# Two banks by turns for the weighted values, six for every other tile, statistics ahead of the constants and more filler matmuls in a two-layer transformer

## Chip, cores and metric

One NeuronCore of one Trainium2 chip (trn2). The metric is the device time of one execution, in microseconds (us), and the median over runs is what counts. The chip's engines are TensorE (PE), VectorE (DVE), ScalarE (ACT), GpSimd (POOL) and SyncE (SP, which here only issues DMAs).

## What is computed

Eight sequences of 1024 tokens, 256 wide, go through two layers, each with 16-head causal attention (heads of 16) and a feed-forward part, all with a residual and a layer norm ahead. Cut to its bones:

```
for layer in (0, 1):
    x = x + softmax(causal(q k^T / 4)) v @ w_out      # q, k, v from layernorm(x); layer 1 also turns q, k (rope)
    x = x + ffn(layernorm(x))
# ffn of layer 0: gates from entmax of 16 logits, z = (x W) * gate, gelu between two such products
# ffn of layer 1: shared squared-relu expert of 128; routed experts only where a gate reaches 1
```

## The kernel before, in words

**Tiles and units.** Tokens are worked in blocks of 512 (c = 0 or 1 of each sequence b), keys in tiles of 128. Attention is cut into 128 units u = (b, layer, group of 4 heads, c), four units to a pass (b, layer, c). For a unit PE first makes scores "s" by query rows (line 1116, with the mask added by a matmul at line 1121 where tiles are packed), DVE takes their maxima (lines 1723 and 1726), POOL splits the maxima into three bf16 parts (line 1651 on), PE turns these ("mt", line 1129), ACT copies them (line 1462) and SP writes them by DMA into the stack of operands. Then PE makes the scores again by key rows, with the maximum subtracted ("st", line 1141), ACT takes the exponential into `probs` (line 1455), POOL cuts the diagonal (line 1630), and PE weighs the values ("pv", line 1159) into one accumulator, `o_bank`. ACT copies this out (line 1468), PE turns it ("nm", line 1167), DVE divides by the sum (line 1745).

**Banks.** PSUM has eight banks of 512 columns. Bank 5 is the accumulator; the other seven (`BANKS`) are a pool, handed to every other tile by turns. `claim` in PE's program waits until the tile that had the bank before is read out (semaphores `drained`). `weigh_values` waits at j = 0 until the copy of the unit before has left the accumulator (`o_drained`). A set-up stage on banks 0 to 4 folds weights (lines 1280 to 1302, with DVE's copies at line 1884) before the attention starts.

**Order.** `program_order` is a planner: it runs over a model of the engines, with a time for each step (`TIMES`), a list of when each bank comes free, at most four "s" tiles and three "st" tiles open, and chooses PE's next step by rank. `LEAD`, `DENSE` and `SPREAD` say when the scores of a coming unit count as late. Steps of the feed-forward chains, of projections (line 1088 and 1096) and of loads go between attention steps. All engines run this one order, each its own part of it.

**Fillers.** Where the model has PE idle (`gap`) before some tiles, the table `FILL` gives the number of dummy matmuls, gap / 0.25, that PE issues into the claimed bank before it waits for the tile's data (`keep_going`, line 1058). Before, this is done for the first tile kinds "xt", "yt", "at" (transposes of x, y and the gates' weights) and for the first "st" of a unit. The profile has 178 fillers.

**The start.** SP issues the first two blocks of x (line 927), with the weights of layer 0 between them, then 3 MB and more of weights that are folded. DVE clears small tiles, fills `vaug` with ones (line 1899), three stacks `stk_k` with -1 (line 1901) and the accumulator with 0 (line 1902), raises `ready0`, and then takes the statistics of both blocks of x ("stat", lines 1692 to 1701). POOL makes the inverse root (line 1593), ACT the normalised x (line 1404), PE its transposes (line 1076), then projections and values, which ACT copies into `vaug` (line 1444), and SP stores and loads the stacks (line 954 on). PE waits for `ready0` at 2 at the end of the set-up stage, ACT at its first copy of values of (0, 0, 0).

Of the kernel before, what the change touches and what calls it, by code (L numbers as in the profile page):

```python
# [10 lines left out]
P = 128  # L11
# [7 lines left out]
DH = D // H  # L19
# [23 lines left out]
PBUF = 4  # L43
PRING = 4
QRING, SRING = 4, 2
O_BANK = 5
LEAD = 9.0
PACE = 0.9
DENSE = 2.0
SPREAD = 1.0  # L50
# [1 line left out]
FOLD_LOADS = 3 + 2 + 10  # L52
SETUP_COPIES = (11, 10)
PACK_S, PACK_T = True, True
BANKS = (0, 1, 2, 3, 4, 6, 7)
SETUP_BANKS = 5
S_MOST, ST_MOST = 4, 3
MARGIN = 2.0
# [174 lines left out]
class Plan:  # L233
# [203 lines left out]
    def weighing_time(self, u, j):  # L437
        b, l, g, c = UNITS[u]
        values = [("v", b, l, j // TPC, tp) for tp in range(TPC // 2)] if g == 0 else []
        if j == key_tiles(c)[-1] and u > 1:  # L440
            values.append(("nm", u - 2))
        if any(item not in self.at for item in values):
            return None
        return max([self.steps[u, j], self.out.get(u - 1, 0.0) if j == 0 else 0.0] + [self.at[item] for item in values])

    def pair_time(self):

# [55 lines left out]
def program_order():  # L503
# [21 lines left out]
    while main or todo or any(plan.chains) or plan.held or plan.outputs:  # L525
# [65 lines left out]
        if can:  # L591
            time, rank, what, args = min(can, key=lambda choice: choice[1])
        else:
            time, rank, what, args = min(choices, key=lambda choice: choice[0])
            plan.pe = max(plan.pe, time) + (0.001 if what == "wait" else 0.0)
            gap += plan.pe - now
        if what == "wait":
            pass
        elif what == "chain":
            item = plan.chains[args[0]][0][0][0]  # L600
            if item[0] in ("xt", "yt", "at") and gap > FILL_TIME:
                FILL[item] = int(gap / FILL_TIME)
            given[args[0]] += plan.give(args[0])
        elif what == "st":
            u, j, h = main.pop(0)
            if j == 0 and h == 0:
                begins[u] = plan.pe
            if j == 0 and h == 0 and gap > FILL_TIME:
                FILL["st", u, j, h] = int(gap / FILL_TIME)
            plan.scores_t(u, j, h)  # L610
            position += 1
            c = UNITS[u][3]
            line = starts[u] + DENSE * unit_work(u) * (j * HG + h + packed_t(j, c)) / (HG * len(key_tiles(c)))
            a, z = query_range(j, c)
            passed += packed_t(j, c) * (2 * (z - a) / 2400 + 0.05)
        else:
            what()
        if what != "wait":
            gap = 0.0

    order = plan.order
# [7 lines left out]
RANK = dict(mt=1, nm=2, burst=3, late=4, st=5, pair=5.5, due=6, s=7, chain=8, single=10)  # L629
EARLY = True  # L630

FILL_TIME = 0.25
FILL = {}

PLACE = {}
# [82 lines left out]
def x_slot(b, c):  # L718
    return (NC * b + c) % X_SLOTS
# [8 lines left out]
def transformer_kernel(nc, x_d, w_qkv_d, w_out_d, proj_d, c1_d, win1_d, wout1_d, c2_d, win2_d, wout2_d,  # L728
# [3 lines left out]
    with ctx:  # L732
# [89 lines left out]

        ps = ctx.enter_context(nc.psum_tensor("ps", [P, 8 * BANK], F32))
        bank = [ps[:, BANK * b:BANK * (b + 1)] for b in range(8)]
        o_bank = bank[O_BANK]
        t_bank = [bank[b] for b in BANKS]

        def sem(name):
# [90 lines left out]
        def _(sp):  # L919
# [20 lines left out]
                sp.dma_start(k2_d[b][l][heads, :, cols].rearrange("h d t -> (h d) t"), src[:, 2]).then_inc(stored, 16)  # L940

            def load_stack(u):
                b, l, g, c = UNITS[u]
                for k in range(c + 1):
                    for w in range(2):
                        parts_in_dram(sp, PROJ["qk", b, l, k, g // 2, w])
                if u >= NBUF:
                    written(sp, last_transposed(u - NBUF, key_tiles(UNITS[u - NBUF][3])[-1]))
                loaded, i, n = stk_loaded[u % NBUF], u % NBUF, BANK * (c + 1)
                heads = slice(HG * g, HG * (g + 1))  # L950
                q = q_d[b][l][heads, :, :, BANK * c:BANK * (c + 1)]
                for r in range(2):
                    rows = slice(ROWS_T * r, ROWS_T * (r + 1))
                    sp.dma_start(stk_q[rows, i], q.rearrange("h d p t -> (d p) h t")).then_inc(loaded, 16)
                    k = k_d[b][l][r, heads, :, :, 0:n].rearrange("h d p t -> (d p) h t")
                    sp.dma_start(stk_k[rows, i, :, 0:n], k).then_inc(loaded, 16)
                sp.dma_start(stk_q[ROWS_A:ROWS_S, i], q[:, :, 0, :].rearrange("h d t -> d h t")).then_inc(loaded, 16)
                k = k2_d[b][l][heads, :, 0:n].rearrange("h d t -> d h t")
                sp.dma_start(stk_k[ROWS_A:ROWS_S, i, :, 0:n], k).then_inc(loaded, 16)
# [86 lines left out]
        def _(pe):  # L1046
# [62 lines left out]
            def score(u, i, h, p):  # L1109
                c, slot = UNITS[u][3], u % NBUF  # L1110
                width = dict(score_parts(i))[p]
                pe.wait_ge(stk_loaded[slot], 16 * STACK_DMAS * (u // NBUF + 1))
                n, (out, done) = packed(width), claim(("s", u, i, h, p))
                for a in range(n):
                    q = stk_q[0:ROWS_S, slot, h + a, P * i - BANK * c:P * (i + 1) - BANK * c]
                    ins = pe.matmul(out[:, width * a:width * (a + 1)], q, stk_k[0:ROWS_S, slot, h + a, BANK * p:BANK * p + width],  # L1116
                                    start=a == 0, stop=a == n - 1 and n == 1)
                if n > 1:
                    last = out[:, 0:n * width].rearrange("q (a w) -> q a w", a=n)[:, :, width - P:width]
                    mask = mask_b[:, BANK - P:BANK].rearrange("q (a w) -> q a w", a=1).broadcast_to([P, n, P])  # L1120
                    ins = pe.matmul(last, ident_b[:], mask, start=False, stop=True)  # L1121
                ins.then_inc(done, 1)

            def max_rows(u):
                pt, done = claim(("mt", u))
                rows = pt[0:NP * HG, 0:BANK // 2].bitcast(BF16)
                pe.wait_ge(mx_ready, u + 1)
                for i in range(TPC):
                    ins = pe.transpose(rows[:, P * i:P * (i + 1)], mparts[:, i].rearrange("q p h -> q (p h)"), ident_b[:])  # L1129
                ins.then_inc(done, 1)  # L1130

            def scores_t(u, j, h):
                c, slot = UNITS[u][3], u % NBUF
                out, done = claim(("st", u, j, h))
                if j == 0 and h == 0:
                    keep_going(("st", u, j, h), out)
                    pe.wait_ge(m_loaded, 16 * (MT["mt", u] + 1))
                a, z = query_range(j, c)
                cols, width = slice(a - BANK * c, z - BANK * c), z - a
                for k in range(packed_t(j, c)):  # L1140
                    ins = pe.matmul(out[:, width * k:width * (k + 1)], stk_k[0:ROWS, slot, h + k, P * j:P * (j + 1)],  # L1141
                                    stk_q[0:ROWS, slot, h + k, cols], start=True, stop=True)
                ins.then_inc(done, 1)

            def weigh_values(u, j):
# [2 lines left out]
                    pe.wait_ge(p_ready, DIAGONAL[u, j])  # L1148
                else:
                    in_sbuf(pe, last_transposed(u, j))  # L1150
                if j == 0 and u:
                    pe.wait_ge(o_drained, u)
                if g == 0 and j % TPC == 0:
                    for tp in range(TPC // 2):
                        in_sbuf(pe, ("v", b, l, j // TPC, tp))
                a, z = query_range(j, c)
                cols, v = slice(a - BANK * c, z - BANK * c), v_slot(b, l, j // TPC)
                for h in range(HG):
                    ins = pe.matmul(o_bank[32 * h:32 * h + DH + 1, cols], vaug[:, v, j % TPC, HG * g + h, :],  # L1159
                                    probs[:, STEP[u, j] % PBUF, h, cols], start=j == 0, stop=j == key_tiles(c)[-1])  # L1160
                ins.then_inc(pv_done, 1)

# [26 lines left out]

            def narrow_product(key, n, b, c, w):
                need_xT(n, b, c)
                pt, done = claim(key)
                for kd in range(KD):
                    for t in range(TPC):
                        ins = pe.matmul(pt[STRIP * t:STRIP * (t + 1), 0:P], w[:, kd, :], xT(n, b, c, kd)[:, P * t:P * (t + 1)],
                                        start=kd == 0, stop=kd == KD - 1)
                ins.then_inc(done, 1)
# [183 lines left out]
        def _(act):  # L1382
# [53 lines left out]
            def copy_v(item):  # L1436
                b, l, c, tp = item[1:]
                old = values_before(b, l, c)
                if old and tp == 0:
                    act.wait_ge(pv_done, PV["pv", LAST_UNIT[old], TT - 1] + 1)  # L1440
                if (b, l, c, tp) == (0, 0, 0, 0):
                    act.wait_ge(ready0, 2)
                pt = arrived(act, item)
                act.activation(vaug[:, v_slot(b, l, c), 2 * tp:2 * tp + 2, :, 0:DH],
# [19 lines left out]
            def copy_o(u):  # L1464
                act.wait_ge(pv_done, PV["pv", u, key_tiles(UNITS[u][3])[-1]] + 1)
                if u >= 2:
                    written(act, ("nm", u - 2))
                act.activation(oT[:, u % 2], o_bank, ACT.Copy).then_inc(o_drained, 1)  # L1468

            last_narrow = []  # L1470

# [207 lines left out]
        def _(dve):  # L1679
# [216 lines left out]
            dve.memset(up, 0.0).then_inc(up_zeroed, 1)  # L1896
            dve.memset(going[:, :, 1:E0], 1.0)
            dve.memset(going[:, :, 0:1], 0.0)
            dve.memset(vaug[:], 1.0)
            for i in range(NBUF):  # L1900
                dve.memset(stk_k[ROWS_A:P, i, :, :], -1.0)
            dve.memset(o_bank, 0.0)
            dve.wait_ge(pool_chain, 8)
            dve.drain().then_inc(ready0, 1)

            for item in ORDER:
                kind, *key = item
                if kind == "stat":
                    b, c = key
                    dve.wait_ge(x_loaded[x_slot(b, c)], 16 * ((NC * b + c) // X_SLOTS + 1))  # L1910
                    statistics(0, c, x[:, x_slot(b, c)], range(TPC))
                elif kind == "rot":
                    swap_pairs(*key)
                elif kind == "setup":
# [86 lines left out]
```

## Time and profile before

| | us |
|---|---|
| median of 3 runs | 3037.79 (3033.26 to 3039.56) |
| the profiled execution | 3033.58, of which the span is 3031.9 |
| PE busy | 2849.9 (94%), 17865 matmuls |
| DVE, ACT, POOL busy | 2074.2 (68%), 1957.8 (65%), 1213.8 (40%) |
| mean granted clock of TensorE | 0.978 |

### The profile page before, as it was taken

The numbers are of one execution on the slowest core, as the hardware profiler recorded it, in microseconds if no ns is written. First come the engines' busy times: TensorE is split into PE (matmuls) and PEld (weight loads), VectorE is DVE, ScalarE is ACT, GpSimd is POOL, SyncE is SP. The second block draws the span as 40 slices with busy tenths as digits, with TensorE's granted clock in tenths as the row PEclk, the third lists the DMA queues.
The fourth block names the chain that finished last, engine by engine and source line by source line (L and its number), as shares of the span: only waits on it lengthen the run. The fifth ranks groups of instructions, "written<-read, shape, count | busy, mean of one in ns | idle before, by whom it ended". The sixth has DMA issues, their size and how long they took to land.

```text
span 3031.9 us, 55430 instructions
## 1 busy us (share of the span) xinstructions
PE 2849.9 (94%) x17865; PEld 1365.7 (45%) x17865; DVE 2074.2 (68%) x5654; ACT 1957.8 (65%) x3868; POOL 1213.8 (40%) x2540
## 2 busy tenths in 40 slices
PE   5898999999999999999999999999999999999987
PEld 3334443445434454445534454344543445444533
DVE  3683677666877678685786758776687767867473
ACT  3465666776657766676667766577666776667544
POOL 2324461445415362263623545143531537225411
PEclk8899999999999999999999999999999999999989
DMA  5612452334423353234522435133442335333140
GB/s 170 147 27 67 97 112 48 86 99 110 98 56 87 93 125 88 55 104 90 143 56 56 128 86 123 38 88 96 114 108 42 96 96 131 71 63 80 45 105 16
DMA packets 241197, 268.27 MB, mean 88 GB/s; under 512 B 19568, under 2 KB 208912, under 8 KB 240912
## 3 DMA queue, kind: packets, MB, share of 16 engines
q1 hardware_dynamic: 240912, 264.66, 36.8%
q8 instruction: 156, 2.56, 0.4%
q14 instruction: 129, 1.06, 0.1%
HBM read 162.35 MB, written 100.66 MB: 87 GB/s over the span
## 4 chain that ended last, share of the span: by engine, by line
PE 70%; DVE 13%; ACT 8%; issue 3%; DMA 3%; SPq 2%; POOL 1%; DVEq 0%; ACTq 0%; POOLq 0%
PE ps L1159 16%; PE ps L1141 13%; PE ps L1116 12%; PE ps L1096 6%; PE ps L1088 6%; DVE mx L1726 5%; ACT probs L1455 4%; PE ps L1237 4%; PE ps L1232 3%; DMA stk_k<-k 3%; DVE ps L1723 2%; PE ps L1224 2%; PE ps L1076 2%; ACT xn L1404 1%; PE ps L1121 1%
## 5 line engine op out<-in xcount | busy, mean ns | idle before, releaser
L1455 ACT ACTIVATE probs<-ps 128x512 f32<-128x512 f32 (+1 forms) x2432 | 1229.4, 587 | 355.7 <-PE ps L1141 349.2
L1726 DVE TENSOR_REDUCE mx<-ps 128x1 f32<-128x512 f32 (+2 forms) x1408 | 886.9, 682 | 240.5 <-PE ps L1116 177.7
L1630 POOL TENSOR_SCALAR_AFFINE_SELECT probs<-probs 128x128 f32<-128x128 f32 (+2 forms) x1408 | 476.1, 345 | 1277.0 <-ACT probs L1455 1247.7
L1723 DVE CUSTOM_DVE_ANT_0 ps<-ps,mask_b 128x512 f32<-128x512 f32 (+1 forms) x1024 | 614.1, 649 | 316.0 <-PE ps L1116 313.5
L1116 PE MATMUL ps<-stk_k,stk_q 112*128 112x512 bf16 (+3 forms) x3072 | 771.5, 333 | 34.5 <-DVE mx L1726 11.7
L1141 PE MATMUL ps<-stk_q,stk_k 115*128 115x512 bf16 (+3 forms) x3072 | 751.4, 328 | 16.7 <-ACT probs L1455 9.2
L1159 PE MATMUL ps<-probs,vaug 128*17 128x512 f32 (+3 forms) x6144 | 580.6, 490 | 15.4 <-POOL probs L1630 10.2
L1141 PEld LDWEIGHTS ps<-stk_q,stk_k 115*128 115x128 bf16 x3072 | 270.6, 97 | 436.4 <-issue 220.1
L1116 PEld LDWEIGHTS ps<-stk_k,stk_q 112*128 112x128 bf16 x3072 | 276.2, 98 | 399.3 <-issue 251.3
L1159 PEld LDWEIGHTS ps<-probs,vaug 128*17 128x17 f32 x6144 | 137.0, 96 | 324.6 <-issue 203.5
L1088 PE MATMUL ps<-turned,wqkv 128*128 128x512 f32 x512 | 263.7, 610 | 6.8 <-ACT turned L1391 3.7
L1404 ACT ACTIVATE xn<-x,shift,rstd 128x256 f32<-128x256 f32 x256 | 138.4, 608 | 56.0 <-POOL shift L1595 56.0
L1615 POOL TENSOR_TENSOR scratch<-scratch,parts 128x512 f32<-128x512 f32 x128 | 148.2, 1158 | 57.2 <-ACT scratch L1422 29.0
L1620 POOL TENSOR_TENSOR parts<-scratch,parts 128x512 bf16<-128x512 f32 x128 | 147.9, 1158 | 47.0 <-ACT parts L1434 47.0
L1750 DVE TENSOR_TENSOR x<-ps,x 128x512 f32<-128x512 f32 x128 | 87.7, 686 | 112.4 <-PE ps L1096 112.3
L1468 ACT ACTIVATE oT<-ps 128x512 f32<-128x512 f32 x128 | 76.8, 600 | 135.2 <-PE ps L1159 135.2
L1391 ACT ACTIVATE turned<-ps 128x512 f32<-128x512 f32 x192 | 115.1, 614 | 60.6 <-PE ps L1175 42.4
L1462 ACT ACTIVATE mT<-ps 12x512 bf16<-12x512 bf16 x128 | 74.1, 579 | 122.2 <-PE ps L1129 122.1
L1482 ACT ACTIVATE scratch<-ps 128x512 f32<-128x512 f32 x128 | 75.3, 596 | 115.5 <-PE ps L1232 115.4
L1237 PE MATMUL ps<-scratch,win 128*128 128x512 f32 x256 | 132.6, 600 | 11.5 <-ACT scratch L1482 11.5
L1723 DVE DVE_READ_ACCUMULATOR2_ANT mx<- 128x1 f32 x1024 | 143.2, 140 | 0.0
L1096 PE MATMUL ps<-wo,turned 128*128 128x256 f32 x512 | 132.0, 386 | 6.6 <-ACT turned L1391 6.6
(153 smaller groups left out, 3005.4 us busy)
## 6 DMA issues: line engine op xcount, KB each, us to landing
k<-parts SPq DMA_DIRECT2D x128, 384.0 KB, 3.4
stk_q<-q SPq DMA_DIRECT2D x256, 192.0 KB, 4.1
stk_k<-k SPq DMA_DIRECT2D x128, 384.0 KB, 6.3
q<-parts SPq DMA_DIRECT2D x64, 384.0 KB, 3.0
stk_k<-k SPq DMA_DIRECT2D x128, 192.0 KB, 4.2
x<-in_L_attn_x SPq DMA_DIRECT2D x16, 512.0 KB, 5.0
k<-parts SPq DMA_DIRECT2D x64, 128.0 KB, 3.4
stk_q<-q SPq DMA_DIRECT2D x128, 64.0 KB, 6.4
```

The source lines that it names most:

```text
L1088: ins = pe.matmul(pt, wqkv[l][:, kd, D * w + P * m:D * w + P * (m + 1)], xT(2 * l, b, c, kd), start=kd == 0, stop=kd == KD - 1)
L1096: ins = pe.matmul(pt[:, D * i:D * (i + 1)], left(kd)[:, cols], right(kd), start=kd == 0, stop=kd == n_k - 1)
L1116: ins = pe.matmul(out[:, width * a:width * (a + 1)], q, stk_k[0:ROWS_S, slot, h + a, BANK * p:BANK * p + width], start=a == 0, stop=a == n ...
L1141: ins = pe.matmul(out[:, width * k:width * (k + 1)], stk_k[0:ROWS, slot, h + k, P * j:P * (j + 1)], stk_q[0:ROWS, slot, h + k, cols], star ...
L1159: ins = pe.matmul(o_bank[32 * h:32 * h + DH + 1, cols], vaug[:, v, j % TPC, HG * g + h, :], probs[:, STEP[u, j] % PBUF, h, cols], start=j ...
L1237: pe.matmul(acc, win2[:, k, :], hsb[k % 3], start=k == 0, stop=k == OC - 1)\
L1404: ins = act.activation(xn[:, t, :], src[:, t, :], ACT.Identity, bias=shift[:, i, t:t + 1], scale=rstd[:, i, t:t + 1])
L1455: act.activation(probs[:, step % PBUF, h:h + k, cols], src, ACT.Exp, scale=SCALE)\
L1615: pool.tensor_tensor(q, q, parts[:, o % PRING, 0], ALU.subtract).then_inc(rest_ready, 1)
L1630: pool.affine_select(out=diag, in_=diag, compare_op=ALU.is_ge, fill=0.0, base=0, pattern=[[0, k]] * (k > 1) + [[1, P]], channel_multiplier ...
L1723: dve.tensor_tensor_reduce(tile, tile, mask_b[:, BANK - width:BANK], 1.0, LOWEST, ALU.add, ALU.max, most)\
L1726: dve.tensor_reduce(most, tile.rearrange("q (k w) -> q k w", k=k), AX.X, ALU.max)\
```

## The change

The accumulator becomes two banks, 5 and 0, by the parity of the unit, and the wait at j = 0 is for the copy of the unit before the last. Bank 0 leaves the pool, which has six. The planner's rule for "pv" follows, and `LEAD` goes from 9 to 10. The constants that DVE writes move into a function that is called behind the statistics of block (0, 1); SP then waits for `ready0` at 2 ahead of the first stack, and ACT at the first values of both blocks. Fillers are planned before nine kinds of tile where the modelled gap is over 0.7 (before: four kinds, over 0.25), with the same division by 0.25; of the nine, "nm" has no `keep_going` in PE's program. In `score` and `narrow_product` the bank is now claimed before the wait for the operands.

```diff
-O_BANK = 5
-LEAD = 9.0
+O_BANKS = (5, 0)
+LEAD = 10.0
-BANKS = (0, 1, 2, 3, 4, 6, 7)
+BANKS = (1, 2, 3, 4, 6, 7)
...
-        return max([self.steps[u, j], self.out.get(u - 1, 0.0) if j == 0 else 0.0] + ...)
+        return max([self.steps[u, j], self.out.get(u - 2, 0.0) if j == 0 else 0.0] + ...)
...
-            item = plan.chains[args[0]][0][0][0]
-            if item[0] in ("xt", "yt", "at") and gap > FILL_TIME:
-                FILL[item] = int(gap / FILL_TIME)
...
-            if j == 0 and h == 0 and gap > FILL_TIME:
-                FILL["st", u, j, h] = int(gap / FILL_TIME)
...
         if what != "wait":
+            item = plan.order[made]
+            if gap > FILL_FROM and item[0] in ("xt", "yt", "at", "st", "mt", "s", "nm", "lg", "rt"):
+                FILL[item] = int(gap / FILL_TIME)
...
-FILL_TIME = 0.25
+FILL_TIME, FILL_FROM = 0.25, 0.7
...
             def load_stack(u):
+                if u == 0:
+                    sp.wait_ge(ready0, 2)
...
             def score(u, i, h, p):
+                n, (out, done) = packed(width), claim(("s", u, i, h, p))
+                keep_going(("s", u, i, h, p), out)
                 pe.wait_ge(stk_loaded[slot], 16 * STACK_DMAS * (u // NBUF + 1))
-                n, (out, done) = packed(width), claim(("s", u, i, h, p))
...
             def max_rows(u):
                 pt, done = claim(("mt", u))
+                keep_going(("mt", u), pt)
...
-                if j == 0 and u:
-                    pe.wait_ge(o_drained, u)
+                if j == 0 and u > 1:
+                    pe.wait_ge(o_drained, u - 1)
...
             def narrow_product(key, n, b, c, w):
+                pt, done = claim(key)
+                keep_going(key, pt)
                 need_xT(n, b, c)
-                pt, done = claim(key)
...
-                if (b, l, c, tp) == (0, 0, 0, 0):
+                if (b, l, tp) == (0, 0, 0):
                     act.wait_ge(ready0, 2)
...
-            dve.memset(vaug[:], 1.0)
-            for i in range(NBUF):
-                dve.memset(stk_k[ROWS_A:P, i, :, :], -1.0)
-            dve.memset(o_bank, 0.0)
-            dve.wait_ge(pool_chain, 8)
-            dve.drain().then_inc(ready0, 1)
+            def fill_constants():
+                dve.memset(vaug[:], 1.0)
+                for i in range(NBUF):
+                    dve.memset(stk_k[ROWS_A:P, i, :, :], -1.0)
+                for pt in o_bank:
+                    dve.memset(pt, 0.0)
+                dve.wait_ge(pool_chain, 8)
+                dve.drain().then_inc(ready0, 1)
...
                     statistics(0, c, x[:, x_slot(b, c)], range(TPC))
+                    if (b, c) == (0, 1):
+                        fill_constants()
```

## Rows read from the trace of the kernel before

**Rows 1.** Mean granted clock, then stretches: PE, PEld, DVE, ACT, POOL busy, PEclk, DMA.
```profile
...
core 0: 3031.9 us, clock 0.978
...
0.00:160.00 160.00, 116.19 (x633) 59.88 (x633) 82.53 (x191) 66.96 (x129) 51.60 (x106) 0.86 0.59 154
160.00:2880.00 2720.00, 2611.28 (x16514) 1255.08 (x16515) 1911.44 (x5265) 1822.28 (x3603) 1137.50 (x2367) 0.99 0.37 86
2880.00:3032.00 152.00, 122.48 (x720) 50.75 (x718) 80.18 (x201) 68.58 (x138) 24.71 (x68) 0.91 0.27 60
...
```

**Rows 2.** Timeline of DVE, start: start, length, engine, line, operation.
```profile
...
2.11 3.69 DVE L1899 MEMSET vaug<- 128x4352 f32 x1 [0.85 <-issue]
...
19.42 1.41 DVE L1692 BATCH_NORM_STATS2 st<-x 128x6 f32<-128x256 f32 x4
...
23.34 0.16 DVE L1701 TENSOR_SCALAR veps<-mv 128x4 f32<-128x4 f32 x1
...
61.11 0.69 DVE L1884 COPY probs<-ps 128x512 f32<-128x512 f32 x1 [37.61 <-PE ps L1280]
...
```

**Rows 3.** Timeline of all engines, start.
```profile
...
0.80 0.46 SPq L927 DMA_DIRECT2D x<-in_L_attn_x  x1
...
1.85 0.47 SPq L927 DMA_DIRECT2D x<-in_L_attn_x  x1
...
17.64 0.60 SPq L990 DMA_DIRECT2D scratch<-in_L_attn_Wv_up  x1
...
27.11 1.97 PE L1076 MATMUL ps<-ident,xn 128*128 128x128 f32 x8 [17.62 <-ACT xn L1404]
...
43.78 0.57 ACT L1444 ACTIVATE vaug<-ps 128x512 f32<-128x512 f32 x1
...
64.88 0.94 SPq L954 DMA_DIRECT2D stk_q<-q  x1
...
```

**Rows 4.** DMA issues of the first 60 us: count, KB each, time to landing.
```profile
...
x<-in_L_attn_x SPq DMA_DIRECT2D x2, 512.0 KB, 5.2
...
```

**Rows 5.** Stretches about the clock's changes, columns as in rows 1.
```profile
...
9.50:27.10 17.60, 0.00 (x0) 0.00 (x0) 12.04 (x24) 2.07 (x4) 1.22 (x2) 0.63 0.51 173
27.10:34.40 7.30, 6.55 (x14) 3.60 (x15) 0.00 (x0) 1.99 (x4) 0.00 (x0) 0.50 0.00 0
82.20:95.90 13.70, 8.71 (x28) 4.49 (x29) 9.28 (x32) 3.85 (x7) 2.05 (x6) 0.50 0.73 171
293.90:307.60 13.70, 8.23 (x26) 2.80 (x27) 13.22 (x59) 2.55 (x5) 2.06 (x6) 0.50 0.31 106
...
860.50:867.30 6.80, 6.80 (x16) 2.50 (x17) 5.80 (x16) 1.68 (x3) 0.00 (x0) 0.50 0.79 152
1222.30:1225.70 3.40, 3.40 (x8) 1.15 (x7) 3.06 (x9) 0.93 (x2) 0.00 (x0) 0.50 1.06 162
...
```

**Rows 6.** Timeline of PE at the seam of units 35 and 36.
```profile
...
855.22 0.41 PE L1159 MATMUL ps<-probs,vaug 128*17 128x128 f32 x8
856.44 0.63 PE L1167 MATMUL ps<-ident,oT 128*128 128x128 f32 x4 [0.81 <-ACT oT L1468]
...
859.27 0.38 PE L1129 MATMUL ps<-ident_b,mparts 128*12 128x128 bf16 x4 [0.84 <-POOL mparts L1654]
860.49 1.02 PE L1210 MATMUL ps<-ident,cum 128*48 128x128 f32 x4 [0.84 <-DVE cum L1822]
...
```

**Rows 7.** PE's waits, 160 to 2880 us: total, times, longest.
```profile
...
PE ps L1141 <- ACT probs L1455: 9.2, 28, 0.9
...
PE ps L1116 <- DVE mx L1726: 7.2, 27, 1.5
...
PE ps L1159 <- POOL probs L1630: 6.5, 8, 1.0
...
PE ps L1116 <- DVE mx L1723: 4.6, 12, 1.5
...
```

**Rows 8.** Timeline of PE near the end: fillers in one place.
```profile
...
3008.44 5.99 PE L1058 MATMUL ps<-mask_b,ident_b 128*128 128x512 bf16 x27
...
```

More of the change, by code:

```diff
@@ L443, in weighing_time @@
             return None
-        return max([self.steps[u, j], self.out.get(u - 1, 0.0) if j == 0 else 0.0] + [self.at[item] for item in values])
+        return max([self.steps[u, j], self.out.get(u - 2, 0.0) if j == 0 else 0.0] + [self.at[item] for item in values])
     def pair_time(self):
@@ L596, in program_order @@
             gap += plan.pe - now
+        made = len(plan.order)
         if what == "wait":
@@ L824, in transformer_kernel @@
         bank = [ps[:, BANK * b:BANK * (b + 1)] for b in range(8)]
-        o_bank = bank[O_BANK]
+        o_bank = [bank[k] for k in O_BANKS]
         t_bank = [bank[b] for b in BANKS]
@@ L1134, in scores_t @@
                 out, done = claim(("st", u, j, h))
+                keep_going(("st", u, j, h), out)
                 if j == 0 and h == 0:
-                    keep_going(("st", u, j, h), out)
                     pe.wait_ge(m_loaded, 16 * (MT["mt", u] + 1))
@@ L1158, in weigh_values @@
                 for h in range(HG):
-                    ins = pe.matmul(o_bank[32 * h:32 * h + DH + 1, cols], vaug[:, v, j % TPC, HG * g + h, :],
+                    ins = pe.matmul(o_bank[u % 2][32 * h:32 * h + DH + 1, cols], vaug[:, v, j % TPC, HG * g + h, :],
                                     probs[:, STEP[u, j] % PBUF, h, cols], start=j == 0, stop=j == key_tiles(c)[-1])
@@ L1467, in copy_o @@
                     written(act, ("nm", u - 2))
-                act.activation(oT[:, u % 2], o_bank, ACT.Copy).then_inc(o_drained, 1)
+                act.activation(oT[:, u % 2], o_bank[u % 2], ACT.Copy).then_inc(o_drained, 1)
             last_narrow = []
```

## The prediction

> **What bounds the kernel now.** I read first the mean granted clock and the span in three stretches [rows 1]: from 160 to 2880 us PE is busy 2611.3 of 2720.0 us, DVE 1911.4, ACT 1822.3. So PE is the bound, and in the long middle only 108.7 us of PE's idle time can be had. The two ends are worse: 43.8 us idle of the first 160, and 29.5 of the last 152. The same rows show the second reserve, the clock: 0.978 over all, 0.86 and 0.91 at the ends and 0.99 between. A share of 0.022 of 3031.9 us is 67 us, and that is what full clock would give back if PE had been busy all through the slow stretches.
>
> Then the timelines of the start. PE's first transpose of x is at 27.11 us, after 17.62 us of idle time that ended with the normalised x [rows 3]. DVE fills constants from 2.11 us and takes its first statistics at 19.42 us [rows 2], though both blocks of x were issued at 0.80 and 1.85 us and take 5.2 us to land [rows 3, 4]. So the statistics wait for DVE's queue, not for data.
>
> Then the clock by stretches [rows 5]. TensorE is at 0.50, which is 1.2 GHz, from 27.10 to 34.40 us, after 17.6 us without a matmul; for 13.7 us from 82.20 and again from 293.90; and once in each sequence's period of about 358 us for 6.8 us, as from 860.50 (3.4 us at 1222.30). There are seven of these dips; the five not shown, from 502.1, 1577.3, 1935.7, 2294.1 and 2652.5 us, are like the one at 860.50. Ahead of that one PE has idle pieces of 0.81, 0.84 and 0.84 us in 6 us, before "nm", before "mt" and before the transposes of the gates [rows 6].
>
> Last, PE's waits in the middle [rows 7]. This is where banks show. PE waits for a bank of the pool to be read out for 9.2 us in 28 waits before "st", and for 7.2 in 27 and 4.6 in 12 before scores: 21.0 us, 67 times, 0.31 us each. The list has 26 kinds of wait, and none is of the value matmuls (line 1159) for the copy of the accumulator (line 1468).
>
> **The change, part by part.** The sum goes by the profiled execution, 3033.6 us.
>
> *Statistics ahead of the constants.* Removed from the path to the first transpose: DVE's stretch from 2.11 to 19.42 us. The new limit is the landing of x: block (0, 0) at 0.80 + 5.2 = 6.0 us, block (0, 1) at 7.05. Both statistics take 19.42 to 23.50 us, 4.1 us [rows 2], so they end at 10.1 instead of 23.5: -13.4 us. What follows (inverse root, normalised x, transposes, projections, set-up) is one chain with no fixed time in it, and the last weights that set-up needs were issued at 17.64 us [rows 3], so I keep all of it. The constants themselves cost 17.3 us from 2.11 to 19.42 and one more bank of about 0.5 us, and end near 10.1 + 17.8 = 28 us. They are costed at nothing. Three covers hide them: DVE's next work is at 61.11 us after 37.61 us of idle time [rows 2]; ACT's first copy of values, behind the new wait, is at 43.78, now 30.4 us; and SP's first load of a stack, also behind the new wait, is at 64.88, now 51 [rows 3]. The nearest cover is ACT's, with 2.4 us to spare; if it is gone, the projections' copies queue behind it, and the cost is 1 to 3 us. Behind SP's wait stand only loads that come later anyway. PE issues the same first fillers, then is idle until about 13.7 us instead of 27.1. Whether the clock still falls is open: at worst the 7.3 us at 1.2 GHz stay, at best 6.55 / 2 = 3.3 us come back [rows 5]. I take 0. **-13.4.**
>
> *Fillers and the clock.* The new kinds are those at which PE idles ahead of the dips, "mt" above all [rows 6]. The idle 0.84 us before "mt" would be filled, the ones before "nm" (which has no filler in PE's program) and before the gates' transposes (where the model may see no gap) would not. The dips cost 6 x 6.8 + 3.4 = 44.2 us at half speed, 22.1 us [rows 5]. Between 0 and -22.1 I take half, -11, since one of three idle pieces goes. The two long stretches at 82 and 294 us have PE busy for 8.7 and 8.2 us at half clock, so at most 8.5 us come back; the 4 to 5 us of idle time at their heads are of kinds that get fillers, and I take -4. At the end, 0.09 of 152 us is 13.7 us of clock, half of it return; many fillers are there already, and the waits are for chains: -2. **-17.**
>
> Against it stand fillers that are too many. One costs 5.99 / 27 = 0.22 us [rows 8]. Where the trace has 0.84 us of idle time and the model should plan 2 us, seven fillers (at 0.25 us planned for each) take 1.55 us and make "mt" 0.7 us late, and behind "mt" on PE stand the gates' transposes, on ACT its copy, on SP the load of the maxima. One such place for each of 7 periods is 5 us; nothing at the least; three such places, 15 us. The old fillers of one or two before a unit's first "st" go, as their gaps are under 0.7. **+5.**
>
> *Two accumulators.* The wait that they loosen does not show in PE's list [rows 7], since the planner already puts other work there: at the seam of units 35 and 36 it makes "nm", scores, "mt" and transposes before any new value [rows 6]. An indirect gain cannot be more than the 6.5 us for which value matmuls wait for POOL. **0**, between -6.5 and 0.
>
> *Six banks in the pool.* The trace has no pool of six. From below: nothing or a small gain, if the new order places the tiles better. From above: the 21.0 us of waits for banks double. The steady need is less than seven: DVE reads a tile in 0.7 us and ACT in 0.6, PE makes one in 0.2 to 0.6, so two or three tiles in flight keep each busy; only bursts want the seventh. I take somewhat less than half of the 21.0. **+9.**
>
> *LEAD* 10 for 9 moves scores a little earlier and is costed at nothing, ±5 us; the bound is the 108.7 us of idle time in the middle, of which it can shift only the part at seams.
>
> Sum: 3033.6 - 13.4 - 17 + 5 + 9 = **3017 us** for a profiled execution. The median of before is 4.2 us above its own profiled execution, with runs on both sides; for a median I put 3018.
>
> **The rivals.**
> *1. Fillers bring nothing.* The pieces before "nm" and the gates' transposes are enough for the clock to fall, or the new order makes its gaps elsewhere. Then 3033.6 - 13.4 + 5 + 9 = 3034. For it: only one of three pieces is filled. Against: with it gone, PE's idle share of these 6 us is down by a third. Chance 0.18.
>
> *2. The pool of six bites; slower.* The place is where a chain holds a bank for long (the sum of eight gelu products, line 1237) while scores and "st" both want three or four. If waits for banks come to four times their number, that is 63 us more instead of 9: 3017 + 54 = 3071. It decides from 32 us on, since 3017 - 9 + 32 is past 3039.7. For it: the planner allows four scores and three "st" open, seven in all, against six. Against: now only 21 us in 2720 are spent so. Chance 0.08.
>
> *3. Turning through fewer banks costs clock.* Each short wait for a bank is an idle piece; if four more places of each period fall to 1.2 GHz for 6.8 us, that is 28 x 3.4 = 95 us, less for stretches where PE idles, say 3017 + 50 to 95 = 3067 to 3112. The trace speaks against it: the 67 waits for banks of the middle stand beside a clock of 0.99 [rows 1, 7]. Chance 0.03. The Trainium skill describes this in "TensorE: Matmul & The Clock Gate", section "A second HAM failure mode: psum-queue depth-cycling": a kernel that cycles through PSUM banks lets PE idle briefly so often that the clock goes up and down. By that rule the change would be slower; by the row it isn't.
>
> *4. All dips go and the accumulators help.* 3033.6 - 13.4 - 3.3 - 22 - 8 - 6 - 6.5 + 3 = 2977; with half of these, 2995. Chance 0.16.
>
> **How the numbers follow.** The forecast has 0.55. Its own range, by the bounds of fillers (0 to 15), banks (0 to 21) and dips (0 to -22), is 3000 to 3032. The range given adds rival 1 and the near half of rival 4, and the first part of rival 2: 2988 to 3040, which leaves out about 2 in 10. A difference of 0.2%, 6 us, is about what a measurement of this kernel can tell from none. Faster by more: the forecast, rival 4 and a third of rival 1: 0.77. Within: the rest of rival 1, 0.12. Slower: rivals 2 and 3: 0.11.
>
> **What would show it.** In the timeline of the start: statistics at 6 to 7 us, the first transpose at 13 to 14, the first copy of values near 30, set-up near 46. If the first transpose has moved by 13 and the middle hasn't gained, rival 1 is right. In the stretches: the seven dips, counted. In PE's waits: the waits of lines 1116 and 1141 for DVE and ACT, 30 us instead of 21; over 50 is rival 2. In the groups: fillers over 178, and what PE's busy time grows by. The forecast is wrong if the first transpose comes later than 16 us, or if the middle, from 160 us on, is longer than before.

## The result

The changed kernel takes 3055.79 us (median of 4 runs, 3051.52 to 3057.53) against 3037.1 for before: ratio 1.006, with a 95% interval of 1.0048 to 1.0072. That is 18.7 us slower, or 0.6%, where 3018 was forecast. The profiled execution took 3055.5 us. Times of experiments below are medians too; with two accumulators, six banks and LEAD 9, one execution of four took 7309.19 us at a mean clock of 0.439 and its ratio leaves that one out.

The mean granted clock and the stretches, as in [rows 1]:

```profile
core 0: 3053.8 us, clock 0.993
...
0.00:160.00 160.00, 133.22 (x753) 66.92 (x753) 94.94 (x221) 80.51 (x156) 55.18 (x117) 0.96 0.59 154
160.00:2880.00 2720.00, 2617.66 (x16371) 1219.76 (x16370) 1872.26 (x5205) 1834.93 (x3559) 1125.16 (x2340) 1.00 0.37 85
2880.00:3054.00 174.00, 142.68 (x830) 60.14 (x826) 90.04 (x231) 77.70 (x156) 37.92 (x85) 0.91 0.28 66
```

The clock is up from 0.978 to 0.993, and in the middle it is 1.00: the seven dips at the seams [rows 5] are gone. By the arithmetic of the prediction that alone should be worth some 20 us. PE's idle time in the middle is 102.3 us, 6 less than before. And yet the whole is slower: from 160 us on it takes 2893.8 us against 2871.9 before, which was the forecast's own sign of being wrong. The time is not in PE's idle column: PE's busy time in the span has grown from 2849.9 to 2893.6 us. The profile has 261 fillers for 178; 83 more at 0.22 us are 18 of these 43.7 us.

The start went as planned. DVE, then PE, as in [rows 2, 3]:

```profile
4.92 1.40 DVE L1696 BATCH_NORM_STATS2 st<-x 128x6 f32<-128x256 f32 x4 [3.65 <-DMA x<-in_L_attn_x]
...
8.37 1.41 DVE L1696 BATCH_NORM_STATS2 st<-x 128x6 f32<-128x256 f32 x4 [1.37 <-DMA x<-in_L_attn_x]
...
10.30 0.16 DVE L1705 TENSOR_SCALAR veps<-mv 128x4 f32<-128x4 f32 x1
11.31 3.69 DVE L1905 MEMSET vaug<- 128x4352 f32 x1 [0.85 <-issue]
...
28.02 1.02 DVE L1909 MEMSET ps<- 128x512 f32 x2
47.54 0.69 DVE L1888 COPY probs<-ps 128x512 f32<-128x512 f32 x1 [18.50 <-PE ps L1284]
```

```profile
3.82 5.57 PE L1059 MATMUL ps<-mask_b,ident_b 128*128 128x512 bf16 x18 [3.82 <-POOL mask_b L1590]
14.08 1.97 PE L1077 MATMUL ps<-ident,xn 128*128 128x128 f32 x8 [4.69 <-ACT xn L1408]
```

Block (0, 0) landed at 4.92 and block (0, 1) at 8.37 us; the statistics are done at 10.5, the first transpose is at 14.08 instead of 27.11. ACT's first copy of values and SP's first load of a stack, in their timelines:

```profile
30.34 0.57 ACT L1448 ACTIVATE vaug<-ps 128x512 f32<-128x512 f32 x1
```

```profile
51.36 0.89 SPq L955 DMA_DIRECT2D stk_q<-q  x1
```

The constants run from 11.31 to 29.04 us, ahead of DVE's next work at 47.54. ACT's first copy of values is at 30.34 (before 43.78), and SP's first load of a stack at 51.36 (64.88): neither waited for the constants. So 13.0 us are won here.

Where are they lost? The copy of the accumulator marks the units. For the 65th and the 81st unit, one period apart, ACT's timeline of the changed kernel and then of before has:

```profile
1531.73 0.60 ACT L1472 ACTIVATE oT<-ps 128x512 f32<-128x512 f32 x1 [2.28 <-PE ps L1162]
...
1895.71 0.60 ACT L1472 ACTIVATE oT<-ps 128x512 f32<-128x512 f32 x1 [2.28 <-PE ps L1162]
```

```profile
1527.65 0.60 ACT L1468 ACTIVATE oT<-ps 128x512 f32<-128x512 f32 x1 [1.71 <-PE ps L1159]
...
1886.39 0.60 ACT L1468 ACTIVATE oT<-ps 128x512 f32<-128x512 f32 x1 [1.71 <-PE ps L1159]
```

A period takes 364.0 us against 358.7, though before spends 3.4 us of its own on a dip. The first period of 16 units loses nothing (the changed kernel is 15.6 us ahead at the first unit and 16.9 at the 17th), the second 10.8 us, and each after it 4 to 6 us. PE's waits in the middle, as in [rows 7], show only part of it:

```profile
PE ps L1118 <- DVE mx L1730: 15.0, 30, 0.9
...
PE ps L1097 <- ACT probs L1459: 7.4, 8, 1.0
PE ps L1162 <- ACT probs L1459: 6.5, 23, 1.5
...
PE ps L1118 <- DVE mx L1727: 4.1, 18, 0.6
PE ps L1118 <- ACT probs L1459: 3.8, 8, 1.3
...
PE ps L1144 <- ACT probs L1459: 3.0, 10, 0.5
...
PE ps L1162 <- POOL probs L1634: 1.5, 4, 0.6
```

The three rows that I had added up, 21.0 us before, are 3.0 + 15.0 + 4.1 = 22.1 here. Waits for a tile that ACT was to read have grown from 1.4 to 3.8 us before scores, and 7.4 before the products of line 1097 are new. Together that is 11 us more; from the first unit to the last, the changed kernel loses 35 us on before. The sign that I had named for rival 2, over 50 us of waits of scores and "st" for DVE and ACT, didn't come: they are 26 us, close to the 30 that I had named for the forecast. Yet, as the experiments show, the mechanism of rival 2 did.

### The profile page after: what moved, and what is told of

Same layout as the page of the kernel before. It is cut to its first block, busy times and chain, and to the rows that moved or that the text cites. A ratio compares the mean times of both kernels' runs of the same rounds, so it can differ in the third digit from the quotient of the medians.

```text
span 3053.8 us, 55605 instructions
## 1 busy us (share of the span) xinstructions
PE 2893.6 (95%) x17948; PEld 1346.8 (44%) x17948; DVE 2057.2 (67%) x5655; ACT 1993.1 (65%) x3868; POOL 1218.3 (40%) x2540
## 4 chain that ended last, share of the span: by engine, by line
PE 66%; DVE 15%; ACT 12%; issue 4%; DMA 2%; POOL 1%; SPq 1%; ACTq 0%; DVEq 0%; POOLq 0%
PE ps L1162 13%; PE ps L1118 11%; PE ps L1144 11%; PE ps L1097 7%; ACT probs L1459 6%; PE ps L1089 6%; DVE mx L1730 5%; DVE ps L1727 4%; PE ps L1241 4%; PE ps L1236 4%; ACT xn L1408 2%; PE ps L1170 2%; PE ps L1228 1%; PE ps L1123 1%; DMA stk_k<-k 1%
## 5 line engine op out<-in xcount | busy, mean ns | idle before, releaser
L1459 ACT ACTIVATE probs<-ps 128x512 f32<-128x512 f32 (+1 forms) x2432 | 1261.8, 585 | 405.4 <-PE ps L1144 392.0
L1144 PE MATMUL ps<-stk_q,stk_k 115*128 115x512 bf16 (+3 forms) x3072 | 762.9, 328 | 15.2 <-DMA stk_q<-mT 5.3
L1162 PE MATMUL ps<-probs,vaug 128*17 128x512 f32 (+3 forms) x6144 | 591.7, 490 | 16.4 <-ACT probs L1459 8.7
L1655 POOL CAST mparts<-mx 128x16 bf16<-128x16 f32 x128 | 26.1, 204 | 561.4 <-DVE mx L1735 290.6
L1746 DVE RECIPROCAL rec<-ps 128x16 f32<-128x16 f32 x128 | 32.6, 255 | 210.1 <-PE ps L1170 199.2
L1395 ACT ACTIVATE turned<-ps 128x512 f32<-128x512 f32 x192 | 115.7, 614 | 78.4 <-PE ps L1077 46.1
L1097 PE MATMUL ps<-wqkv,turned 128*128 128x256 f32 x512 | 130.8, 384 | 2.9 <-DVE mx L1727 2.1
```

What stands on the lines that cost most here:

```text
L1097: ins = pe.matmul(pt[:, D * i:D * (i + 1)], left(kd)[:, cols], right(kd), start=kd == 0, stop=kd == n_k - 1)
L1162: ins = pe.matmul(o_bank[u % 2][32 * h:32 * h + DH + 1, cols], vaug[:, v, j % TPC, HG * g + h, :], probs[:, STEP[u, j] % PBUF, h, cols], s ...
L1459: act.activation(probs[:, step % PBUF, h:h + k, cols], src, ACT.Exp, scale=SCALE)\
```

## The experiments

Each ran beside the kernel before, whose median was 3035.1, 3035.0, 3035.6 and 3034.8 us in the four groups. Ratios have intervals of about ±0.0015.

### Each part alone

**Statistics first.** Before with `fill_constants` behind the statistics of (0, 1), and the two waits on `ready0`:

```diff
                     statistics(0, c, x[:, x_slot(b, c)], range(TPC))
+                    if (b, c) == (0, 1):
+                        fill_constants()
```

> The kernel before with the constants moved behind the first statistics and nothing else. Theory (this is a clean gain that is kept, the loss is elsewhere): the unit marks of the changed kernel stood 15.6 us ahead of before at the first unit, so this kernel is 13 to 16 us faster than before, about 3022, and the distance to before stays constant over all units. Rival (an earlier start is lost later on, to colliding loads): first unit 15 us ahead, the end less than 5 us ahead.

3021.4 us, ratio 0.9956 (0.9942 to 0.997): -13.7. The distance at the copies of the accumulator is 13.8 us at the first unit and 11.8 at the last. The gain is kept.

**The rule of fillers.** Before with

```diff
+            if gap > FILL_FROM and item[0] in ("xt", "yt", "at", "st", "mt", "s", "nm", "lg", "rt"):
+                FILL[item] = int(gap / FILL_TIME)
```

and `keep_going` where the change has it; `score` and `narrow_product` also claim their bank before the wait for the operands, as in the change.

> The kernel before with the new rule of fillers and nothing else: its own order and seven banks, LEAD 9. Theory (fillers pay): the seven dips of the clock in the middle go, which gives at most 22 us, and too many fillers cost some back: 5 to 20 us faster, 3017 to 3032. Rival (the changed kernel's loss of about 5 us per period from unit 16 on is PE time taken by fillers): as slow as the changed kernel or slower, over 3050, with PE's busy time up by 40 us.

3011.3 us, ratio 0.9926 (0.9909 to 0.9942): -23.8. The profile has weight loads for 324 fillers instead of 178, and rows for 295 of their matmuls; 29 are missing in it. The stretch of the middle, and the seam of [rows 6] in PE's timeline:

```profile
160.00:2880.00 2720.00, 2619.21 (x16666) 1262.23 (x16688) 1916.38 (x5288) 1825.89 (x3610) 1142.67 (x2372) 1.00 0.37 88
```

```profile
849.64 0.41 PE L1160 MATMUL ps<-probs,vaug 128*17 128x128 f32 x8
...
850.86 0.63 PE L1168 MATMUL ps<-ident,oT 128*128 128x128 f32 x4 [0.81 <-ACT oT L1470]
...
853.37 1.46 PE L1057 MATMUL ps<-mask_b,ident_b 128*128 128x512 bf16 x6 [0.52 <-DVE mx L1728]
854.76 0.39 PE L1130 MATMUL ps<-ident_b,mparts 128*12 128x128 bf16 x4
855.08 0.62 PE L1212 MATMUL ps<-ident,cum 128*48 128x128 f32 x4
...
859.63 0.81 PE L1142 MATMUL ps<-stk_q,stk_k 115*128 115x512 bf16 x3
```

The fillers (seven by their weight loads, six in this row) end at 854.83 us, and "mt" starts 5.12 us after the last value matmul, where it was 4.05 before: 1.1 us late, as feared. But the clock stays at 1.00, and the first "st" of the next unit comes 9.99 us after the last value matmul. Before it had come 12.14 us after:

```profile
867.36 0.81 PE L1141 MATMUL ps<-stk_q,stk_k 115*128 115x512 bf16 x3
```

By the copies of the accumulator, some 17 of the 22.2 us that are won at the last unit come in the four units that begin at each of the seven seams (2.3 to 3.3 us each, 1.4 where the dip had been 3.4 us), 2.0 before the 17th unit and 1.7 in the last eight. The idle 0.81 us before "nm", where no filler stands, is still there, and 0.52 us stand before the fillers, until DVE has read the tile that had their bank; the piece before the gates' transposes is gone, since a late "mt" takes its place. So one set of fillers took most of two of the three pieces.

**Only ahead of "mt".** The same with

```diff
-            if gap > FILL_FROM and item[0] in ("xt", "yt", "at", "st", "mt", "s", "nm", "lg", "rt"):
+            if gap > FILL_FROM and item[0] in ("xt", "yt", "at", "mt"):
```

> The kernel before with fillers before the tile kinds xt, yt, at and, new, mt, by gaps over 0.7; none before s, st, lg, rt. If the fillers ahead of mt are what keeps the clock at the seams: most of the 23.8 us of the whole rule, 3012 to 3020, no dip at the seven seams. Rival (those before scores do it): 3027 to 3035.

3012.4 us (0.992, 0.9904 to 0.9937). The fillers ahead of "mt" bring practically all: -23.2 of -23.8. Six seams have no dip, and seven fillers each. The seventh, where this kernel issues none, keeps 3.4 us at half speed, half of this stretch (clock 0.75):

```profile
502.10:508.90 6.80, 6.80 (x20) 2.76 (x18) 5.44 (x14) 1.93 (x4) 0.00 (x0) 0.75 0.77 145
```

No run tells whether the clock stays because idle time is filled or because of the fillers' own work.

**Banks, accumulators and LEAD 10 without the rest.**

```diff
-O_BANK = 5
-LEAD = 9.0
+O_BANKS = (5, 0)
+LEAD = 10.0
-BANKS = (0, 1, 2, 3, 4, 6, 7)
+BANKS = (1, 2, 3, 4, 6, 7)
...
-        return max([self.steps[u, j], self.out.get(u - 1, 0.0) if j == 0 else 0.0] + ...)
+        return max([self.steps[u, j], self.out.get(u - 2, 0.0) if j == 0 else 0.0] + ...)
...
-                if j == 0 and u:
-                    pe.wait_ge(o_drained, u)
+                if j == 0 and u > 1:
+                    pe.wait_ge(o_drained, u - 1)
...
```

> The kernel before with two accumulators, six banks in the pool and LEAD 10, the old rule of fillers, the constants where they were. Theory (the six banks are the loss, and the new rule of fillers and the early statistics each gave some of it back): 3056 + 15 for the start + 10 to 25 for the clock = 3080 to 3095, with the dips of the clock present. Rival (the fillers are the loss): about 3045, near before.

3081.2 us (1.015, 1.0133 to 1.0167): +46.1, as the first theory had it. This is the part that makes the change slower.

**The changed kernel with the old rule of fillers.**

```diff
-            if gap > FILL_FROM and item[0] in ("xt", "yt", "at", "st", "mt", "s", "nm", "lg", "rt"):
-                FILL[item] = int(gap / FILL_TIME)
...
+            if item[0] in ("xt", "yt", "at") and gap > FILL_TIME:
+                FILL[item] = int(gap / FILL_TIME)
...
+            if j == 0 and h == 0 and gap > FILL_TIME:
+                FILL["st", u, j, h] = int(gap / FILL_TIME)
```

> The changed kernel with the rule of fillers of before. Theory (fillers pay in the changed kernel too): slower than the changed kernel by 10 to 25 us, 3066 to 3080, with a mean clock near 0.98 instead of 0.993. Rival (fillers cost): faster than the changed kernel, 3035 to 3050.

3053.3 us: both theories miss. The clock of this kernel is at 1.00 in the middle already:

```profile
160.00:2880.00 2720.00, 2604.16 (x16279) 1216.95 (x16309) 1871.18 (x5203) 1834.12 (x3560) 1121.36 (x2343) 1.00 0.36 85
```

It has no dip at a seam, so the new rule had none to take away: 3055.8 against 3053.3 is +2.5, inside the scatter of both. The rule does act: the mean clock is 0.993 with it and 0.988 without, which is some 30 us less at half speed, nearly all of it before 300 us. But it issues 261 fillers for 171, and PE's busy time is 2893.6 us against 2876.9. The fillers are worth 24 us in the order of before and nothing in the order of six banks.

**The change without its banks**: the edits of the first two experiments together, seven banks, LEAD 9.

> The kernel before with early statistics and the new rule of fillers, seven banks, LEAD 9: what the change is without its banks. If the two parts add up (-13.7 and -23.8 alone): 3035 - 37 = 2998. If part of the fillers' gain was clock that early statistics also move: 3002 to 3010.

2997.4 us (0.9875, 0.9859 to 0.9892). The two parts add up, -37.6. A period of this kernel:

```profile
1506.96 0.60 ACT L1472 ACTIVATE oT<-ps 128x512 f32<-128x512 f32 x1 [1.71 <-PE ps L1162]
...
1863.17 0.60 ACT L1472 ACTIVATE oT<-ps 128x512 f32<-128x512 f32 x1 [1.71 <-PE ps L1162]
```

356.2 us, against 358.7 before and 364.0 in the changed kernel.

**With fillers before "nm" too.**

```diff
                 out, done = claim(("nm", u))
+                keep_going(("nm", u), out)
```

> Early statistics and the new rule of fillers on seven banks (2997 us), with the fillers that the table plans before nm really issued (57 more). The clock in the middle is at 1.00 without them, so they can only cost: 0 to 8 us slower, 2997 to 3005. Rival (they cover idle time at the ends as well): 2 to 5 us faster.

2996.8 us (0.987, 0.9853 to 0.9886): the same as without.

### What the banks cost

A planned kernel mixes two things: fewer banks, and the order that the planner then writes. So the order was kept and only the dealing changed. A function walks over the finished order and gives every tile the bank that the planner's own times have free first:

```diff
-    PLACE.update(plan.place)
+    BANKS[:] = [1, 2, 3, 4, 6, 7]
+    PLACE.update(dealt(order, plan.at))
```

**The control**, dealt anew over the same seven (the line that sets `BANKS` names all seven).

> Control: the kernel before, order kept, tiles dealt anew over the same seven banks by the same small function that dealt them over six in the run that came to 3161 us. If the way of dealing costs nothing: 3030 to 3042, as before. If it costs, the 126 us of the six banks hold that cost too.

3035.4 us, ratio 1.0 (0.999 to 1.0009). The function costs nothing.

**Before's order on six banks, one accumulator.**

> The kernel before, its order of all work kept instruction by instruction, one accumulator, but its tiles dealt over six banks in place of seven (bank 0 unused), each to the bank that the planner's own times have free first. It tells the banks from the order. Theory A (six banks hold up any order: PE waits for drained banks): 40 us or more slower than before, over 3075, with PE's waits before scores and st more than doubled. Theory B (the loss is in the order that the planner makes when it has six banks): at most 20 us slower, under 3056.

3161.0 us (1.0411, 1.0394 to 1.0428): +126. Against the control nothing but the number of banks differs. From the page of its profile, and from that of before:

```profile
span 3159.8 us, 55402 instructions
## 1 busy us (share of the span) xinstructions
PE 2934.1 (93%) x17836; PEld 1354.1 (43%) x17865; DVE 2074.0 (66%) x5654; ACT 1980.3 (63%) x3868; POOL 1213.2 (38%) x2540
```

```profile
span 3031.9 us, 55430 instructions
## 1 busy us (share of the span) xinstructions
PE 2849.9 (94%) x17865; PEld 1365.7 (45%) x17865; DVE 2074.2 (68%) x5654; ACT 1957.8 (65%) x3868; POOL 1213.8 (40%) x2540
```

PE's waits on six banks, 160 to 2880 us, as in [rows 7] (line 1147 is scores, 1172 is "st"):

```profile
PE ps L1147 <- ACT probs L1486: 20.5, 68, 1.4
PE ps L1172 <- ACT probs L1486: 18.8, 41, 0.8
PE ps L1147 <- DVE mx L1754: 10.1, 38, 1.8
...
PE ps L1147 <- DVE mx L1757: 8.1, 25, 1.4
...
PE ps L1172 <- DVE mx L1757: 5.1, 19, 0.5
```

These five are 62.6 us. The same kinds of wait come to 25.2 us before: 1.4 and 9.2 for ACT, 4.6 and 7.2 before scores and 2.8 before "st" for DVE. By the copies of the accumulator the loss is about 1 us per unit: from the 17th unit to the 113th, on the mean 3.8 to 4.9 us in each quarter of a period.

Only a third of the loss can be seen as idle time of PE: the span grew by 127.9 us, PE's idle time by 43.7 and its busy time by 84.2, for the same work at the same clock (0.977 against 0.978; 29 matmul rows, all of fillers, are missing in the first page, so its busy time is rather higher). A matmul's row is longer than its turn: a filler's row lasts 0.38 us (median), and 27 of them take 5.99 us [rows 8], 0.22 each. So a wait that is shorter than the overlap can be counted as busy. The score matmuls of 512 columns bear this out: their mean row is 386 ns on six banks and 387 before, yet together they cover 519.2 us against 505.5. Loads of weights have shorter rows, 97 or 98 ns, and show more of the waits. The groups of loads before scores and "st", first on six banks, then before:

```profile
L1147 PEld LDWEIGHTS ps<-stk_k,stk_q 112*128 112x128 bf16 x3072 | 270.7, 98 | 514.6 <-issue 400.7 <-DMA stk_k<-k 15.9 <-ACT wout2T L1527 0.8
L1172 PEld LDWEIGHTS ps<-stk_q,stk_k 115*128 115x128 bf16 x3072 | 264.9, 97 | 462.3 <-issue 203.9 <-ACT probs L1486 107.0 <-DVE mx L1757 26.0
```

```profile
L1116 PEld LDWEIGHTS ps<-stk_k,stk_q 112*128 112x128 bf16 x3072 | 276.2, 98 | 399.3 <-issue 251.3 <-DMA stk_k<-k 21.2 <-ACT wout2T L1496 0.8
L1141 PEld LDWEIGHTS ps<-stk_q,stk_k 115*128 115x128 bf16 x3072 | 270.6, 97 | 436.4 <-issue 220.1 <-ACT probs L1455 71.5 <-DVE mx L1726 14.0
```

Before scores the idle time of the loads grew from 399.3 to 514.6 us, and before "st" the part that ended with ACT's reading of an earlier tile from 71.5 to 107.0.

**The same with two accumulators.**

```diff
-O_BANK = 5
+O_BANKS = (5, 0)
...
-                if j == 0 and u:
-                    pe.wait_ge(o_drained, u)
+                if j == 0 and u > 1:
+                    pe.wait_ge(o_drained, u - 1)
```

> The order of the kernel before, kept, tiles dealt over six banks (3161 us with one accumulator), now with two accumulators. My prediction said that the second accumulator gives 0 to 6.5 us, as no value matmul waits for the copy of the accumulator: 3154 to 3163. Rival (its worth lies in the waits that it takes away in any order): 3110 to 3140.

3162.1 us: nothing. In the order of before the second accumulator is worth nothing, as PE's waits had said.

**The changed kernel's order on seven banks, one accumulator.** The planner still plans for six banks and two accumulators; then:

```diff
-    PLACE.update(plan.place)
+    BANKS[:] = [0, 1, 2, 3, 4, 6, 7]
+    PLACE.update(dealt(order, plan.at))
...
-                if j == 0 and u > 1:
-                    pe.wait_ge(o_drained, u - 1)
+                if j == 0 and u:
+                    pe.wait_ge(o_drained, u)
```

> The changed kernel, its order kept, with fillers and early statistics, but one accumulator and its tiles dealt over seven banks. Theory A (real waits for banks): the seventh bank gives 20 us or more back, under 3036. Theory B (the order itself is longer): within 10 us of the changed kernel, 3046 to 3066. If the second accumulator is worth something in this order, it comes out slower than the changed kernel.

3021.0 us (0.9956, 0.994 to 0.9973), 34.8 less than the changed kernel, clock 0.994. So more than the loss is real waiting for banks. This order was made for two accumulators, and with one the value matmuls wait for its copy, which they do nowhere in before:

```profile
L1193 PE MATMUL ps<-probs,vaug x6144: 272/590/959, 88.7 to 2982.6; 128*17 128x512 f32 x98, 128*17 128x128 f32 x38, 128*17 128x256 f32 x33, 128*17 128x384 f32 x30
...
  ACT oT L1503: 16.8, 7
```

16.8 us in 7 waits. Against 2997.4 for before's order with the same fillers and statistics it is 23.6 us longer, and these waits may be most of that; no run takes them away alone.

### Planned anew

**Six banks, one accumulator, LEAD 10.**

```diff
-LEAD = 9.0
+LEAD = 10.0
-BANKS = (0, 1, 2, 3, 4, 6, 7)
+BANKS = (1, 2, 3, 4, 6, 7)
```

> The kernel before planned for six banks in the pool and one accumulator (bank 0 unused), LEAD 10, old rule of fillers. Beside the run with two accumulators, six banks and LEAD 10 (3081 us) it prices the second accumulator alone. My prediction priced it at 0 to 6.5 us gain: then this is 3081 to 3090. Rival (the planner needs it to order the seams): 3110 or more.

3131.4 us (1.0318, 1.0301 to 1.0336). Where the planner may use it, the second accumulator is worth 3131.4 - 3081.2 = 50 us.

**Seven banks, LEAD 10.**

```diff
-LEAD = 9.0
+LEAD = 10.0
```

> The kernel before with LEAD 10 and nothing else, seven banks. If LEAD is worth nothing: 3030 to 3041. If LEAD 9 suits the order of seven banks as LEAD 10 that of six: 3045 to 3070.

3079.2 us (1.0148, 1.0131 to 1.0165): +43.6 for one constant.

**The changed kernel at LEAD 9**, the edit above turned round.

> The changed kernel with LEAD 9 in place of 10. My prediction priced LEAD at nothing, 5 us either way: then 3050 to 3061. Rival (with six banks the order hangs on LEAD, which is why it was changed too): over 3080.

3129.2 us (1.0312, 1.0295 to 1.0329): 73 more than at LEAD 10.

**Two accumulators, six banks, LEAD 9**: the experiment that came to 3081.2 us, without its line on LEAD.

> Two accumulators and six banks at LEAD 9, planned, without early statistics and new fillers. The changed kernel at LEAD 9 came to 3129; if the other two parts give their 14 and 0 to 24 us here: 3143 to 3167. Then LEAD 9 to 10 is worth 60 to 85 us with six banks, and costs 44 with seven.

3165.5 us (1.0429, 1.0408 to 1.045). Its clock is 0.972, with 22 stretches at half speed between 160 and 2880 us, 106 us in all, against nine and 61 us before; the 44 us more cost at most half of that, 22 of the 131 us. The square, without the other two parts:

| | LEAD 9 | LEAD 10 |
|---|---|---|
| seven banks, one accumulator | 3035 | 3079 |
| six banks, one accumulator | 3161 (order of before) | 3131 |
| six banks, two accumulators | 3165 | 3081 |

## Why the prediction was wrong

**Statistics ahead of the constants, -13.4.** Right: -13.7 alone. All three covers held; in the changed kernel the nearest, ACT's copy of values, had 1.3 us where 2.4 was reckoned. Block (0, 1) landed later than its 5.2 us (at 8.37, not 7.05), block (0, 0) earlier.

**Fillers and the clock, -17 + 5.** The mechanism was right and its size too small in the order of before: -23.8, since the fillers of one place take away most of two idle pieces of three and with them all seven dips, not half of them, and the late "mt" costs less than the clock gives back. But the term was summed as if the new order had the seams of the old one. It had none of the dips left to save, so in the changed kernel it is 0 (+2.5, within scatter). What clock the rule still gave back there brought no time; the 90 more fillers may have taken it. I read the dips' seams in [rows 6] and then let another part of the same change rewrite them.

**Two accumulators, 0.** Right for the order of before (3162.1 against 3161.0), wrong for this program: an order that may use the second bank is 50 us shorter at LEAD 10. A bound taken from a wait list holds for the order that made the list.

**Six banks, +9.** This step failed worst: +126 in a fixed order, +52 when planned with LEAD 10 and one accumulator. Two mistakes made it. The waits in PE's list, 21.0 us, were taken as the whole of what banks cost, and doubled at most; in the fixed order two thirds of the loss is booked as busy time. (Of the same kind the list also has 2.8 us before "st", 1.7 before line 1096 and 1.4 before scores, 26.9 in all.) And the argument of two or three tiles in flight for DVE and ACT looked at each engine alone, while scores, "st" and a chain may want their tiles together; no run shows how many tiles are wanted at once. Rival 2 named the shortage, with 54 us more and a chance of 0.08; the chance was the error. Its place, the chain of gelu products, was wrong too: in the fixed order the loss is spread evenly over the units.

**LEAD, 0 within 5.** Wrong: +43.6 with seven banks, -84 with six and two accumulators. It is no small constant: it rewrites the order, and of the two values 9 fits seven banks and 10 fits six with two accumulators.

These three terms, banks, accumulators and LEAD, stood at +9 in the sum and measure +46.1 together. They can't be priced one by one: at LEAD 10 the steps are +43.6 for LEAD, +52 for the bank and -50 for the accumulator, at LEAD 9 banks and accumulators together cost 131.

The sum by what was measured: -13.7 for the start, +46.1 for banks, accumulators and LEAD together, 0 to 2.5 for fillers, or 3035.1 + 33 = 3068 to 3070. The chip gave 3055.8, so 13 us are left over. They lie between the kernel with banks alone (3081.2) and the changed kernel with the old fillers (3053.3), which differ by 27.9 us where the early start gives 13.7. At the copies of the accumulator the second is ahead by 13.1 us at the first unit, 17.8 at the 17th, 20.3 at the 25th and 27.8 at the last. Between 160 and 2880 us the first has 37 us at half speed, in eight pieces, the second 14 us in two, both before 300 us; at most 12 us can come of that. So the clock could account for most of the rest; why it differs between two kernels with one order is not known. The bank's claim ahead of the wait for operands in `score` is another candidate. Neither was tried alone, and this stays open.

Rival 1 (fillers bring nothing, because the new order has its gaps elsewhere) holds in the changed kernel, together with rival 2. Rival 3 did not come: the clock was at 1.00 in the middle. Its mechanism isn't ruled out for other orders, as the short stretches at half speed of the kernel with LEAD 9, six banks and two accumulators show, but there too it is the smaller part of the loss. The range was also narrower than its own terms: fillers of 0 to 15, banks of 0 to 21 and dips of 0 to -22 give 2992 to 3050 us, not 3000 to 3032. The measured 3055.8 lies outside both.

## What to carry to other kernels

A wait list prices a resource only at the margin of the present order; to price a buffer, keep the order and take one away. That costs one run, and here it would have said 126 us; of this, planning anew for six banks wins back a part (3131.4 with one accumulator, 3081.2 with two). Where a planner writes the order, every constant of it is a part of the change and must be tried alone. Measured alone, the two other parts were good: without its banks the change gives 2997.4 us, 1.25% faster than before, and this is the version to keep of those measured.

## What was not expected of the hardware

The same matmuls in the same order at the same clock take 2849.9 busy us with seven banks and 2934.1 with six: PE's busy time in the profile holds short waits, and a busy share of 93% (six banks) against 94% (seven) says little of how full PE is. And seven fillers of 0.22 us ahead of one step kept TensorE at 2.4 GHz over a seam where before it fell to 1.2 GHz for 6.8 us, though 0.81 and 0.52 us of idle time stood beside them unfilled.
